# Attention of a two-layer adaLN kernel: causal mask and division by the sums moved to GpSimd

## The reference

```python
q = (x @ Wq + bq).reshape(B, T, H, D)
kv_latent = jax.nn.gelu(x @ Wkd + bkd, approximate=False)
lat = kv_latent[..., :L] + kv_latent[..., L:]
kv = lat @ Wku + bku
attn = jnp.einsum('bqhd,bkhd->bhqk', q, k) * scale
attn = jnp.where(causal, attn, -jnp.inf)
attn = jax.nn.softmax(attn, axis=-1)
out = jnp.einsum('bhqk,bkhd->bqhd', attn, v).reshape(B, T, C)
return out @ Wo + bo
```

## Time and profile before

| what | value |
|---|---|
| median of 3 runs | 786.89 us (788.62, 786.89, 724.57) |
| profiled execution | 727.6 us |
| its span, first to last instruction | 725.8 us |
| mean granted clock of TensorE | 0.93 |
| busy: PE, DVE, ACT, POOL | 631.4, 579.9, 477.5, 200.9 us |

### The profile page before, as it was taken

One profiled execution on the slowest core, in us unless ns is written; L12 is line 12 of the kernel. 1 busy time (PEld: TensorE's weight loads), 2 busy tenths in 40 slices (PEclk: granted clock), 3 DMA queues, 4 the chain that ended last, 5 costly groups with the idle time before them and its releaser, 6 DMA issues.

```text
span 725.8 us, 11354 instructions
## 1 busy us (share of the span) xinstructions
PE 631.4 (87%) x3252; PEld 435.9 (60%) x3252; DVE 579.9 (80%) x1400; ACT 477.5 (66%) x843; POOL 200.9 (28%) x160
## 2 busy tenths in 40 slices
PE   8689899999997899999999995755997988999983
PEld 5355555555545578888888883332665855666762
DVE  2669999999866668888888977649897788888887
ACT  5438888888644579999999994594452534444441
POOL 3400000000002315455435434201422133444423
PEclk9679999999996999999999999785997999999996
DMA  6000000000000212102222100000000321111111
GB/s 224 30 0 2 2 2 0 0 0 0 1 1 0 89 61 88 61 28 87 87 88 87 59 21 0 23 0 0 1 0 4 139 80 65 72 58 60 66 59 58
DMA packets 6796, 30.88 MB, mean 43 GB/s; under 512 B 906, under 2 KB 1043, under 8 KB 4435
## 3 DMA queue, kind: packets, MB, share of 16 engines
q1 hardware_dynamic: 6756, 30.42, 11.6%
HBM read 29.23 MB, written 1.19 MB: 42 GB/s over the span
## 4 chain that ended last, share of the span: by engine, by line
PE 52%; DVE 25%; issue 11%; ACT 10%; DVEq 1%; DMA 1%; POOL 0%; ACTq 0%; SPq 0%
PE PS L1051 10%; PE PS L1053 10%; PE PS L1052 10%; DVE AR L1021 6%; DVE STAT L741 5%; ACT RA L576 4%; PE PS L1166 2%; PE PS L1064 2%; PE PS L1128 2%; DVE HN L600 2%; PE PS L1193 2%; PE PS L1148 2%; PE PS L1073 2%; PE PS L1162 2%; PE PS L1127 1%
## 5 line engine op out<-in xcount | busy, mean ns | idle before, releaser
L297 POOL TENSOR_TENSOR AR<-AR 128x512 f32<-128x512 f32 x68 | 100.9, 1483 | 228.2 <-DVE AR L687 227.6
L875 DVE TENSOR_TENSOR RA<-AR,RA 128x512 fp32r<-128x512 f32 x140 | 135.3, 992 | 29.7 <-ACT RA L481 28.8
L480 ACT ACTIVATE AR<-PS,BI 128x512 f32<-128x512 f32 x144 | 99.5, 691 | 23.9 <-PE PS L1053 14.0
L1051 PE MATMUL PS<-HH,WH 128*128 128x512 f32 x272 | 108.8, 400 | 1.5 <-DVE AR L1021 1.5
L1052 PE MATMUL PS<-HH,WL 128*128 128x512 f32 x272 | 107.8, 396 | 0.0
L1053 PE MATMUL PS<-HL,WH 128*128 128x512 f32 x272 | 107.7, 396 | 0.0
L1051 PE MATMUL PS<-RA,WH 128*128 128x512 f32 x208 | 86.9, 418 | 17.9 <-DVE RA L1028 17.2
L576 ACT ACTIVATE RA<-AR 128x512 fp32r<-128x512 f32 x64 | 40.5, 633 | 89.9 <-DVE AR L1021 89.9
L481 ACT ACTIVATE RA<-PS,BI 128x512 fp32r<-128x512 f32 x144 | 98.4, 684 | 0.0
L1028 DVE TENSOR_TENSOR RA<-AR,RA 128x512 fp32r<-128x512 f32 x64 | 72.2, 1128 | 27.6 <-ACT RA L576 24.7
L1053 PE MATMUL PS<-RA,WH 128*128 128x512 f32 x208 | 82.2, 395 | 0.0
(11 more groups left out here) (183 smaller groups left out, 1197.7 us busy)
## 6 DMA issues: line engine op xcount, KB each, us to landing
AR<-comb SPq DMA_DIRECT2D x17, 1024.0 KB, 4.6
WS<-in_w SPq DMA_DIRECT2D x9, 512.0 KB, 5.5
WS<-in_w SPq DMA_DIRECT2D x8, 384.0 KB, 4.9
M<-in_mats SPq DMA_DIRECT2D x1, 1384.0 KB, 12.1
X<-in_xT SPq DMA_DIRECT2D x4, 256.0 KB, 4.4
out_xT<-X SPq DMA_DIRECT2D x4, 256.0 KB, 2.1
AR<-in_wmod SPq DMA_DIRECT2D x1, 768.0 KB, 9.0
KM<-in_kmats SPq DMA_DIRECT2D x1, 160.0 KB, 9.5
```

The costliest lines, as they stand in the source:

```text
L297: gp.tensor_tensor(out=blk(ACC, t), in0=blk(ACC, t), in1=YW[:, t % 2, :], op=ALU.add)\
L480: act.activation(G[:, c, :], PS[:, c, :], ACT.Gelu_apprx_tanh, bias=bias).then_inc(s["act"], 1)
L875: dve.tensor_tensor(out=GL[:, m0 % 2, c, :], in0=G[:, c, :], in1=f(GH[:, m0 % 2, c, :]), op=ALU.subtract).then_inc(s["lo"], 1)
L1051: pe.matmul(out, wh, xh, start=first, stop=False)
```

## The change

The mask matmuls L1166 and the mask MKK go. In their place GpSimd sets the probabilities above the diagonal to zero behind the exponentials (`causal`): four selections a unit, each over two heads by a diagonal block of 128 columns. TensorE's `values` waits for them in place of the exponentials. GpSimd also takes over the multiplication by the reciprocal sums (`divide`), two units behind. VectorE's `spread_max` writes the rounded maxima into MP directly, which is now of the rounded type, and takes the remainder against MP itself. `spread_sum` now waits for the evacuation and for the buffer. GpSimd's 32 steps stand in its queue ahead of the split of the first expert's weights. The joins stay as they are.

```diff
-        MKK = sb("MKK", [128, 128], bf16)
...
-        MP = sb("MP", [128, 2, 128])
+        MP = sb("MP", [128, 2, 128], r32)
...
+            def causal(n, n0):
+
+                for h in range(2):
+                    gp.wait_ge(exp_done, 2 * n + h + 1)
+                    own = PR[:, n0 % 2, 2 * h:2 * h + 2, :]
+                    for first in (0, 256):
+                        p = own[:, :, first:first + 128]
+                        ins = gp.affine_select(out=p, in_=p, compare_op=ALU.is_ge, fill=none, base=0,
+                                               pattern=[[0, 2], [1, 128]], channel_multiplier=-1)
+                    ins.then_inc(causal_done, 1)
+
+            def divide(n):
+
+                gp.wait_ge(rsx_done, n + 1)
+                gp.tensor_tensor(out=ON[:, n % 4, n // 4 * SEQ:n // 4 * SEQ + SEQ], in0=OT[:, n % 2, :],
+                                 in1=SU[:, n % 2, :], op=ALU.mult).then_inc(on_done, 1)
+
+            none = gp.to_reg(0.0)
+            for n in range(UNITS):
+                causal(n, n)
+                if n >= 2:
+                    divide(n - 2)
+            divide(30)
+            divide(31)
             gp.wait_ge(moe[0]["w_in"], 16)
             split_weights(0, 0, 0, 1024)
...
                 dve.wait_ge(max_done, 4 * n + 4)
-                dve.tensor_copy(NMH, NM[:, :]).then_inc(nmh_done, 1)
-                dve.wait_ge(nmh_done, n + 1)
                 if n0 >= 1:
                     dve.wait_ge(mt_done, n)
-                dve.tensor_copy(MP[:, :, 24::32], f(NMH).rearrange("p (q j) -> p q j", q=2)).then_inc(mp_ready, 1)
-                dve.tensor_tensor(out=MP[:, :, 25::32], in0=nmv, in1=f(NMH).rearrange("p (q j) -> p q j", q=2),
+                dve.tensor_copy(MP[:, :, 24::32], nmv).then_inc(mp_ready, 1)
+                dve.wait_ge(mp_ready, 2 * n + 1)
+                dve.tensor_tensor(out=f(MP[:, :, 25::32]), in0=nmv, in1=f(MP[:, :, 24::32]),
                                   op=ALU.subtract).then_inc(mp_ready, 1)
...
             def spread_sum(n, n0):
-                if n0 == 0:
-                    dve.wait_ge(ot_done, n + 1)
+                dve.wait_ge(ot_done, n + 1)
+                if n0 >= 2:
+                    dve.wait_ge(on_done, n - 1)
                 dve.stream_shuffle(SU[:, n0 % 2, :], OT[:, n0 % 2, :], [16] * 32).then_inc(su_done, 1)
...
-                if n0 >= 3:
-                    divide(n - 3, n0 - 3, it)
...
                     pe.matmul(PS[:, bank, 0:256], KX[r, g, 0:128], QM[r, n0 % 2, :], start=True, stop=False)
-                    pe.matmul(PS[:, bank, 256:384], KX[r, g, 128:256], QM[r, n0 % 2, 128:256],
-                              start=False, stop=False)
-                for j in range(2):
-                    mm = pe.matmul(diagonal(2 + 2 * h + j), IDB[:, :], mask(MKK), start=False, stop=True)
+                    mm = pe.matmul(PS[:, bank, 256:384], KX[r, g, 128:256], QM[r, n0 % 2, 128:256],
+                                   start=False, stop=True)
                 mm.then_inc(st_done, 1)
 
             def values(n, n0, it):
-                pe.wait_ge(exp_done, 2 * n + 2)
+                pe.wait_ge(causal_done, 2 * n + 2)
```

More of the change, by code:

```diff
@@ L104, in build @@
         KR = RA[:, 2816:3072]
-        NMH = RA[:, 3072:3080]
         MASKED_S = STAT[:, 0:1024].rearrange("p (q j n) -> p q j n", q=2, j=2)
@@ L144, in build @@
             sem, ("kd_done", "lat_done", "v_psum", "vall_done", "ones_done"))
-        (proj_done, qk_evac, qx_ready, s_done, max_done, nmh_done, mp_ready, mt_done, qm_ready, st_done,
+        (proj_done, qk_evac, qx_ready, s_done, max_done, mp_ready, mt_done, qm_ready, st_done,
          exp_done, pv_done, ot_done, su_done, ls_done, rsx_done, on_done, vx_ready, wo_done) = map(
-            sem, ("proj_done", "qk_evac", "qx_ready", "s_done", "max_done", "nmh_done", "mp_ready",
+            sem, ("proj_done", "qk_evac", "qx_ready", "s_done", "max_done", "mp_ready",
                   "mt_done", "qm_ready", "st_done", "exp_done", "pv_done", "ot_done", "su_done",
@@ L150, in build @@
         l1_split = sem("l1_split")
+        causal_done = sem("causal_done")
         bias_done = sem("bias_done")
@@ L245, in _ @@
             gp.memset(OND[:, :], 1.0 / D).then_inc(const_done, 1)
-            for m in (IDF, IDB, MQ, MKK, MP):
-                gp.memset(m[:], 0.0).then_inc(ident_done, 1)
-            gp.wait_ge(ident_done, 5)
+            for m in (IDF, IDB, MQ, MP):
+                gp.memset(f(m[:]) if m is MP else m[:], 0.0).then_inc(ident_done, 1)
+            gp.wait_ge(ident_done, 4)
             for m in (IDF, IDB):
@@ L254, in _ @@
                              pattern=[[-1, 128]], channel_multiplier=1).then_inc(ident_done, 1)
-            gp.affine_select(out=MKK[:, :], in_=MKK[:, :], compare_op=ALU.is_ge, fill=MASKED, base=0,
-                             pattern=[[1, 128]], channel_multiplier=-1).then_inc(ident_done, 1)
             for b0 in range(2):
@@ L819, in _ @@
             dve.tensor_scalar(SP[:, 3:4], SP[:, 3:4], -8.0, None, ALU.mult).then_inc(sp_done, 1)
-            dve.wait_ge(ident_done, 9)
+            dve.wait_ge(ident_done, 7)
             dve.wait_ge(in_rows, 32)
@@ L840, in _ @@
                 step(n)
-            divide(29, 29, 0)
             spread_sum(30, 30)
@@ L844, in _ @@
             centre(1, 1)
-            divide(30, 30, 0)
             spread_sum(31, 31)
             centre(1, 2)
-            divide(31, 31, 0)
             normalise(1, 0)
@@ L1201, in maxima_t @@
                 for q in range(2):
-                    mm = pe.transpose(PS[:, 7, 256 + 128 * q:384 + 128 * q], MP[:, q, :], IDF[:, :])
+                    mm = pe.transpose(PS[:, 7, 256 + 128 * q:384 + 128 * q], f(MP[:, q, :]), IDF[:, :])
                 mm.then_inc(mt_done, 1)
@@ L1235, in _ @@
                     mm.then_inc(v_psum, 1)
-            pe.wait_ge(ident_done, 9)
+            pe.wait_ge(ident_done, 7)
             pe.wait_ge(mod_done, 2)
```

## The result

| | before | after |
|---|---|---|
| time, median of the runs compared (us) | 725.6 | 760.79 |
| profiled execution (us) | 727.6 | 760.12 |
| its span (us) | 725.8 | 758.4 |
| mean granted clock of TensorE | 0.930 | 0.827 |

The change makes the kernel slower: the ratio on record is 1.0494, with a 95% interval of 1.0459 to 1.0529. Of the 59 executions of the kernel before on record 21 took 783 to 790 us, at a mean granted clock of 0.82 to 0.83 where one is recorded; no trace of one was taken, every ratio leaves them out, and 725.6 is the mean of the other two of these four (724.57 and 726.66).

The account below looks back on a forecast made before the run. It took the bound to be each attention unit's path: maxima, spreading, TensorE's transposes, addition of the maxima, maxima, joins. 727.6 + 17.4 - 1.9 - 1.4 + 2.4 = 744 us, 2.3% slower; range 732 to 772.

Parts of the forecast that it names:

- Rival 1: Attention: TensorE, busy about 65% without masks, loses its clock to 1.2 GHz and becomes the bound; 765 us, chance 0.20.
- part 2: Attention, TensorE: removing the mask matmuls gives 0 in 28 steps and 1.9 us less in the last three.
- Part 4: Attention units: VectorE's copy, subtraction and joins wait for GpSimd instructions; period 5.35, +0.62 us a unit, 17.4 us in all.
- Part 3: Attention, GpSimd: four selections of 0.40 and a multiplication of 0.66, 2.3 of 4.73 us a unit; GpSimd not the bound.
- Part 1: Attention, VectorE: the division's going gives 0; the shorter spreading takes 0.08 us a unit off the path.
- Part 5: First expert's weight split, moved behind the last multiplication: gain of 1.4 us before the attention, cost of 2.4 after it.
- Rival 2: Attention: no collision between VectorE and GpSimd, period 4.65, 724.5 us, no change; chance 0.08.
- rival 4: Attention: GpSimd's instructions at their upper bound or keeping the port from one to the next; 754 us, chance 0.06.
- Rival 3: Attention: long runs are the rule, TensorE bounds them, removing masks takes 26 off 787; 761 us, 3.3% faster, chance 0.14.

Follow-up runs that it names:

- run 2: Kernel before with the mask matmuls left out, nothing in their place and nothing on GpSimd in the attention; median 756.76 us.
- run 1: Changed kernel with the mask matmuls put back on TensorE, selections and multiplication staying on GpSimd; median 723.56 us.
- run 5: Kernel before with only the shorter spreading of the maxima; ratio 0.9968, median 723.94 us.
- run 8: Changed kernel with eight matmuls, their result overwritten, put ahead of each projection; ratio 0.9978.
- run 3: Changed kernel with the division put back on VectorE, selections still on GpSimd, no masks on TensorE; median 761.65 us.
- run 6: Kernel before with only the first expert's weight split moved behind the last division; ratio 0.9954.
- run 7: Changed kernel with four matmuls, their result overwritten, put ahead of each projection; 748.75, 755.08, 770.93 and 773.51 us.
- run 9: Changed kernel with the mask matmuls put back on TensorE but the mask matrix all zeros; ratio 0.9991.

## Why the prediction was wrong

The sign was right and the range held the time, but for a reason that was given 0.20. Point by point:

- **Rival 1 is what happened.** It was rejected with "PE is short of work for a part of each unit only". That rejection, and with it part 2's price of 0, was the failing step: the start of the attention left TensorE busy for 79%, more than the 65% that the rival worked out, and the clock went all the same. Its time, 765, is 4 us from the median, in part by luck, since it was worked out from the 787 us, whose cause no trace shows. The rows to weigh were the earlier trace rows (3.40 of 6 us busy, then 0.58) beside the earlier trace rows: 20.4 us of masks in 120 were a sixth of the stretch.
- **Part 2** priced the masks as work that hides, 0 in 28 steps, because "PE waits for VectorE anyway". Ahead of the transposes it doesn't: at 2.4 GHz their going takes 0.17 us from three units of four (run 2). What it left out altogether is what their going does to the engine's clock: all of the +37.1.
- **Part 4, the main term**, was 0.62 us a unit, 17.4 in all. At 1.2 GHz, where the changed kernel ran, it was 0. At 2.4 GHz with the masks on TensorE it was 0.09 (4.82 in run 1 against 4.73 in run 5), 2.5 in all. The 4.83 of run 8 is not a collision: there the subtraction ends at 120.89 and the transposes start at 121.14, 0.62 us after the projection's second pair, as in run 5; the eight matmuls hold that projection back longer than the masks do. The mechanism is as predicted: the copy and the subtraction do wait for the selection under way. By the Trainium skill, "SBUF — State Buffer", section "Who interferes with whom", a copy in a two-port mode takes the lock too; the trace agrees (L776, 0.34 beside a selection, 0.17 alone). Two things failed in the working. First, the order of events. A unit of run 8, where the exponentials start 0.87 us behind the join (119.23; drawn 0.72):
```profile
118.36 0.48 DVE L749 SCALAR_TENSOR_TENSOR RA<-QT,V,RA 128x256 fp32r<-128x256 f32 x1
...
120.10 1.48 POOL L319 TENSOR_SCALAR_AFFINE_SELECT AR<-AR 128x256 f32<-128x256 f32 x4 [0.24 <-ACT AR L437]
120.38 0.17 DVE L773 CAST MP<-NM 128x8 fp32r<-128x8 f32 x1
...
120.59 0.30 DVE L775 TENSOR_TENSOR MP<-NM,MP 128x8 f32<-128x8 f32 x1
```
  The copy comes 2.02 us behind the join, to the hundredth as drawn. But the selections start at 1.74, not 1.61, so the copy meets the end of the first and not the whole of the second, and is through in 0.17; only the subtraction waits, 0.13. Drawn were 0.39 and 0.36. Second, the path. The prediction read the 0.87 us from L755 to L762 as a round trip. With the masks in TensorE's queue the transposes stand behind the projection (run 1 against run 5), and most of the waiting is in its shadow. Without them the drawn path is the right one (run 2), and what the collisions then cost at 2.4 GHz can be read only from run 3, whose clock came back from 200.3 to 211.5 us (0.96 there; selections on GpSimd, division on VectorE):
```profile
203.61 0.48 DVE L739 SCALAR_TENSOR_TENSOR RA<-QT,V,RA 128x256 fp32r<-128x256 f32 x1
...
205.84 0.30 DVE L765 TENSOR_TENSOR MP<-NM,MP 128x8 f32<-128x8 f32 x1
...
206.19 0.44 PE L1210 MATMUL PS<-IDF,MP 128*128 128x128 f32 x2 [0.51 <-DVE MP L765]
...
208.22 0.48 DVE L739 SCALAR_TENSOR_TENSOR RA<-QT,V,RA 128x256 fp32r<-128x256 f32 x1
...
210.24 0.39 DVE L763 CAST MP<-NM 128x8 fp32r<-128x8 f32 x1
210.66 0.32 DVE L765 TENSOR_TENSOR MP<-NM,MP 128x8 f32<-128x8 f32 x1
...
211.04 0.67 PE L1210 MATMUL PS<-IDF,MP 128*128 128x128 f32 x2 [0.75 <-DVE MP L765]
```
  The first unit takes 4.61 us, 0.05 more than run 2 without selections. In the second the selections start at 1.62 and the copy ends at 2.41, both as drawn, but the subtraction starts at 2.44, not 2.98; the transposes come 2.82 us behind the join, in the first unit 2.58. That would make some 4.85 (an estimate from these distances, since the clock falls before the unit has ended), where 5.35 was taken. So even with the clock held part 4 was too large.
- **Part 3**: selections 0.41 us (taken 0.40), right; the multiplication 0.74 to 0.86 (taken 0.66), longer.
- **Part 1**: 0.08 us a unit taken, 0.02 measured (run 5), since the transposes stand behind the projection there. That the division's going gives nothing was right.
- **Part 5**: head -1.4 taken, -3.2 in run 6. The term counted only the two halves beside L277; but the split's first half, 22.14 to 23.22, follows GpSimd's earlier work without a gap, so it also holds the two halves ahead of them. The changed kernel's 5.0 is more than the split gives. Most of the rest is there before the split could matter: VectorE's copy of the modulation (L717, L696 in the kernel before) starts at 13.93 in place of 15.58, and over the thirteen traces that copy starts anywhere from 13.4 to 16.1. Tail +2.4 taken, +1.0 to +1.6 measured. In the kernel after, the split and the normalisation beside it:
```profile
244.88 1.05 POOL L271 TENSOR_SCALAR WH<-WS 128x1024 fp32r<-128x1024 f32 x1
246.01 2.67 POOL L274 TENSOR_TENSOR WL<-WS,WH 128x1024 fp32r<-128x1024 f32 x1
```
```profile
246.50 2.65 DVE L621 TENSOR_SCALAR HN<-HN,MC,MOD 128x256 f32<-128x256 f32 x2
```
- **Rival 2** (nothing collides, 724.5) and **rival 4** fell. **Rival 3** named 761 us, the time that came, but as a gain on 787, and that is luck. Run 7 shows only that work added to TensorE at 1.2 GHz is on the path.

## What to carry to other kernels

Before you take "hidden" work from TensorE, ask whether that work holds the granted clock where it is; a run with useless matmuls in its place tells at once. Ask also what stands behind it in the engine's queue, for work that looks hidden may hold back the next thing that another engine waits for. Price a collision not by the instruction that is delayed but by who waits for its result, and whether that one's own queue is free by then. An engine at 98% (VectorE here) need not be the bound: two engines that wait for each other in turn can both look full, and less work for one moves nothing.

## What the runs showed of the hardware

- In the kernel after, the granted clock fell to 0.50 at 49.0 us, and in the 6.80 us before TensorE's longest wait was 0.77 us (at 47.47, for the subtraction). At 0.50 the engine is shown as busy without a gap (36.00 of 36.00 us in run 2), and the clock came back only at times: for 3.8 us in the kernel after, 11 us in run 3, 17 us twice in run 2. What decides that wasn't found. By the Trainium skill, "TensorE: Matmul & The Clock Gate", section "Part 1: The HAM clock gate", the clock follows how busy the engine has been of late. Runs 7 and 8 agree in that the amount of work decided; a "busy" of 36.00 of 36.00 us at 0.50 shows that the profile's busy time is not that measure.
- Matmuls whose result is overwritten (run 8) or whose matrix is all zeros (run 9) hold the clock as the masks do: all twenty runs have a mean clock of 0.937 or more.
- All 57 runs of the seven versions that have the shorter spreading and the masks, the zeros or the eight matmuls have a mean clock of 0.934 or more; with the old spreading, run 6 lost the clock in one run of seven. Whether the shorter spreading helps to hold it is not shown.
- A copy of 8 values a row waits for GpSimd's selection to end: 340 ns in the median of 25, at least 334 (run 1), where its median alone is 171 to 176 (kernel before, run 5). In run 8, where it meets only a selection's end, it is 175.
